# One block for attention and experts, with four row buffers

## The reference, cut to what matters

```
xn = layernorm(x)
s  = attention(xn)        # two causal softmaxes per head, subtracted with weight lambda; RMS norm; @ wo.T
g  = silu(experts(xn))    # top 2 of 8: gate/up (256 -> 512), clipped, gated, down (256 -> 256), weighted sum
out = x + s * g
```

## Time and profile before

| | us |
|---|---|
| median of three runs | 1023.85 (1023.36 to 1024.76) |
| the profiled execution, its own time | 1022.34 |
| its span, first to last instruction | 1020.6 |
| block 1, to about | 160 |
| attention, to the last copy of its results | 743.2 |
| experts, to the last ys (L1684) | 974.95 |
| last stage, to | 1020.6 |

### The profile page before, as it was taken

How to read it: one execution, slowest core, us unless ns; L and a number is a source line. 1 busy time by engine, 2 the same in 40 slices (tenths; PEclk the granted TensorE clock), 3 DMA queues, 4 the chain that set the end, 5 groups by cost and what they waited for, 6 DMA issues and landing times.

```text
span 1020.6 us, 23981 instructions
## 1 busy us (share of the span) xinstructions
PE 907.0 (89%) x6614; PEld 641.3 (63%) x6614; DVE 886.8 (87%) x1743; ACT 768.3 (75%) x2011; POOL 283.0 (28%) x481
## 2 busy tenths in 40 slices
PE   4999985889989899989988898898879999999987
PEld 3877763666666666666666666666646665555676
DVE  6687867999999999999999999999848887778847
ACT  3545435999999999999999999999835555464443
POOL 3000001323332333333200000001146666656610
PEclk9999995999999999999999999999989999999999
DMA  6989966485667758575685556474013333333278
GB/s 209 334 317 314 288 249 187 100 190 139 144 153 173 166 116 185 140 149 139 141 109 125 122 106 141 86 151 92 7 54 120 113 113 99 107 97 106 79 229 287
DMA packets 89553, 157.54 MB, mean 154 GB/s; under 512 B 19580, under 2 KB 48764, under 8 KB 89468
## 3 DMA queue, kind: packets, MB, share of 16 engines
q1 hardware_dynamic: 80544, 137.56, 52.2%
q0 software_dynamic: 8960, 19.41, 6.3%
HBM read 104.57 MB, written 52.36 MB: 154 GB/s over the span
## 4 chain that ended last, share of the span: by engine, by line
PE 33%; DVE 23%; ACT 13%; issue 12%; ACTq 1%; another core or an unknown queue 0%; DVEq 0%; DMA 0%; POOL 0%; POOLq 0%
PE bank L1461 11%; DVE Pr_long L1241 7%; DVE nmax L1191 7%; PE bank L1021 6%; PE bank L1487 5%; ACT Pr_long L1124 4%; DVE nmax L1209 4%; ACT Pr_short L1138 4%; ACT AT L1151 3%; PE bank L1062 2%; PE bank L1528 2%; PE bank L1447 1%; PE bank L1474 1%; PE bank L1023 1%; DVE nmax L1203 1%
## 5 line engine op out<-in xcount | busy, mean ns | idle before, releaser
L1191 DVE TENSOR_REDUCE nmax<-bank 128x1 f32<-128x1024 f32 (+3 forms) x256 | 259.9, 1015 | 5.8 <-PE bank L1023 5.8
L1124 ACT ACTIVATE Pr_long<-bank,nmax 128x1024 f32<-128x1024 f32 (+3 forms) x256 | 252.2, 985 | 9.9 <-DVE nmax L1191 9.8
L1151 ACT COPY AT<-bank 128x512 f32<-128x512 f32 (+3 forms) x384 | 177.3, 494 | 4.3 <-PE bank L1062 2.4
L1021 PE MATMUL bank<-Ks_first,Qs_first 128*128 128x512 f32 (+3 forms) x384 | 123.9, 412 | 28.1 <-ACT Pr_short L1138 18.6
L1138 ACT ACTIVATE Pr_short<-bank,nmax 128x128 f32<-128x128 f32 (+3 forms) x256 | 138.5, 541 | 10.1 <-DVE nmax L1209 2.6
L892 POOL COPY VO<-Ob 128x64 f32 (+1 forms) x128 | 30.2, 236 | 414.3 <-ACT Ob L1160 413.9
L1062 PE MATMUL bank<-ident,Pr_long 128*128 128x128 f32 x832 | 127.9, 280 | 18.3 <-DVE Pr_long L1241 18.2
L1461 PE MATMUL bank<-gu_sb,xsT 128*128 x284 | 135.8, 601 | 4.5 <-ACT xsT L1549 2.7
L1021 PE MATMUL bank<-Ks_second,Qs_second 128*128 128x512 f32 (+3 forms) x384 | 119.2, 399 | 20.7 <-ACT Pr_short L1138 18.5
L1241 DVE SCALAR_TENSOR_TENSOR Pr_long<-Pr_long,coef 128x1024 f32<-128x1024 f32 (+3 forms) x128 | 137.4, 1074 | 0.0
L1023 PE MATMUL bank<-maskb,identb 128*128 128x128 bf16 x512 | 117.8, 233 | 0.0
(11 more groups left out here) (171 smaller groups left out, 1607.3 us busy)
## 6 DMA issues: line engine op xcount, KB each, us to landing
q_parts<-PARTS SPq DMA_DIRECT2D x32, 512.0 KB, 3.1
k_parts<-PARTS SPq DMA_DIRECT2D x32, 512.0 KB, 3.9
Qs_first<-q_parts SPq DMA_DIRECT2D x64, 256.0 KB
Ks_first<-k_parts SPq DMA_DIRECT2D x64, 256.0 KB
Qs_second<-q_parts SPq DMA_DIRECT2D x64, 256.0 KB
Ks_second<-k_parts SPq DMA_DIRECT2D x64, 256.0 KB
X<-x SPq DMA_DIRECT2D x8, 512.0 KB, 5.6
xn_dram<-XN SPq DMA_DIRECT2D x8, 512.0 KB, 6.5
```

The lines of the kernel that those rows point to most:

```text
L1021: nc.tensor.matmul(at[:, c0:c1], Qs[head][:, m, q * P:(q + 1) * P], Ks[head][:, m, c0:c1], start=True, stop=(c1 < N))
L1124: nc.scalar.activation(long_probs(p)[:, m, 0:N], long_slot[m][:, 0:N], ACT.Exp, bias=nmax[:, 4 * p + m:4 * p + m + 1], scale=1.0, accum_ou ...
L1151: nc.scalar.copy(AT[u % 6][:, 0:w], tb[u % BANKS][:, 0:w]).then_inc(unit_out, 1)
L1191: nc.vector.tensor_reduce(nmax[:, 4 * p + m:4 * p + m + 1], long_slot[m][:, 0:N], AX.X, ALU.max, negate=True).then_inc(long_maxed, 1)
```

## The change

- `no_rows` is laid out for four buffers: its iota writes 18 partitions of 8192 words instead of 36 of 4096. It and the iota of `row_ids` move behind GpSimd's other constants.
- Blocks 2 and 3 become one block. The code of block 3 moves into functions (`experts_sp`, `experts_pool`, `experts_pe`, `experts_act`, `experts_dve`) that are called where each engine's attention code ends; their bodies are the same but for what follows.
- In the last iteration TensorE turns the rows of tiles 0 and 1 behind pair 5's frame, runs gate_and_up(0) behind pair 6's and gate_and_up(1) behind pair 7's; ScalarE copies both tiles' turned rows behind pair 6's frame and runs the first gate_curve behind pair 7's. GpSimd fetches the rows of tiles 1 to 3 behind its copy for pair 5.
- Four buffers `xs` and four `ys` in the place of two; AHEAD is 7. A store of ys is waited for four tiles later, and not at all for the first four; the two dummy loads go.
- d1e is computed in the step of tile 1. The Silu table is loaded behind the first three `turned_out`.

The diff, cut; lines that only move are left out.

```diff
-AHEAD = 5
+AHEAD = 7
+ROW_BUFS = 4
+Y_ROWS = TOP_K * T + ROW_BUFS * P
...
-            no_rows = sb("no_rows", [SLOT_TILES // 2, 2 * P, ID_WORDS], I32, where=ph)
+            no_rows = sb("no_rows", [SLOT_TILES // ROW_BUFS, ROW_BUFS * P, ID_WORDS], I32, where=ph)
...
                     nc.gpsimd.tensor_copy(identb[:], ident[:]).then_inc(consts_done, 1)
-                    nc.gpsimd.iota(no_rows[:], pattern=[[1, 2 * P], [0, ID_WORDS]], base=TOP_K * T, channel_multiplier=0
-                                   ).then_inc(no_rows_ready, 1)
-                    nc.gpsimd.iota(row_ids[:], pattern=[[P, NT], [T, TOP_K]], base=0, channel_multiplier=1
-                                   ).then_inc(no_rows_ready, 1)
...
                     nc.gpsimd.tensor_scalar(count_128, count_f[:, 0:T // P], float(P), None, ALU.mult
                                             ).then_inc(consts_done, 1)
+                    nc.gpsimd.iota(no_rows[:], pattern=[[1, ROW_BUFS * P], [0, ID_WORDS]], base=TOP_K * T, channel_multiplier=0
+                                   ).then_inc(no_rows_ready, 1)
+                    nc.gpsimd.iota(row_ids[:], pattern=[[P, NT], [T, TOP_K]], base=0, channel_multiplier=1
+                                   ).then_inc(no_rows_ready, 1)
...
                 for p in range(NP):
                     frame(NIT - 1, p)
+                    behind(p)
...
+            xs = [xs_first] + [sb(f"xs{u}", [P, D], where=ph) for u in range(1, ROW_BUFS)]
...
+            ys = [sb(f"ys{u}", [P, D], where=ph) for u in range(ROW_BUFS)]
...
+                    def rows_in(n):
+
+                        if n >= ROW_BUFS:
+                            pool.wait_ge(xs_turned, 2 + n - ROW_BUFS + 1)
+                        u = n % ROW_BUFS
+                        pool.indirect_dma_start(xs[u][:], None, xn_dram, bass.IndirectOffsetOnAxis(
+                            slot_tokens[:, n:n + 1], 0)).then_inc(xs_loaded[u], 16)
+
+                    if begin:
+
+                        pool.wait_ge(long_scored, credited(NIT - 1, 2 * NP, 2 * NP - 1))
+                        pool.wait_ge(short_scored, credited(NIT - 1, 2 * NP, 2 * NP - 1))
+                        for n in range(1, ROW_BUFS):
+                            rows_in(n)
+                        return
...
+                def first_rows_turned(pe):
+                    pe.wait_ge(ew_loaded, 64 * E)
+
+                    pe.wait_ge(long_exped, credited(NIT - 1, 2 * NP, 2 * NP - 1))
+                    turn_rows(0, 0)
+                    turn_rows(0, 1)
+
+                def experts_pe(pe, load):
+
+                    pe.wait_ge(short_exped, credited(NIT - 1, 2 * NP, 2 * NP - 1))
+                    pe.wait_ge(unit_out, credited(NIT - 1, UNITS, UNITS - 1))
+                    turn_rows(0, 2)
+                    turn_act(0, 0)
+
+                    pe.wait_ge(o_out, credited(NIT - 1, NP, NP))
...
+                    run_steps(pe, step, load, begun=True)
...
+                    for c in range(W_SETS):
+                        turned_out(c)
+
+                    nc.scalar.activation(silu_table[:], ident[:, 0:1], ACT.Silu)
...
+                    m = 2 * it + u
+                    if m == 0:
+                        nc.vector.wait_ge(pv_done, credited(NIT - 1, NP, NP))
+                    if m >= ROW_BUFS:
+                        nc.vector.wait_ge(y_stored[m % ROW_BUFS], 16 * (m // ROW_BUFS))
...
                             pool.indirect_dma_start(xs_first[:], None, xn_dram, bass.IndirectOffsetOnAxis(
                                 slot_tokens[:, 0:1], 0)).then_inc(xs_loaded[0], 16)
+                        if p == 5:
+                            experts_pool(pool, True)
...
                     keep_rows(NIT - 1, NP)
+                    experts_pool(pool, False)
...
+                    def behind(p):
+
+                        if p == NP - 3:
+                            first_rows_turned(pe)
+                        if p == NP - 2:
+                            first.append(load(0))
+                            gate_and_up(0, 0, first[0])
+
+                    run_pairs(pe, 4, frame, behind)
+                    gate_and_up(0, 1, first[0])
                     pe.wait_ge(o_out, credited(NIT - 1, NP, NP - 1))
                     sum_rows(NP - 1).then_inc(pv_done, 1)
+                    experts_pe(pe, load)
...
+                    def behind(p):
+                        if p == NP - 2:
+                            first_rows_out(act)
+
+                    run_pairs(act, 4, frame, behind)
+                    gate_curve(0, 0)
                     act.wait_ge(pv_done, credited(NIT - 1, NP, NP))
                     act.wait_ge(o_kept, credited(NIT - 1, NP, NP - 2))
                     nc.scalar.copy(Ob[0][:, P:], ob[:, P:P + 2 * DH]).then_inc(o_out, 1)
+                    experts_act(act)
```

792 lines of the change are left out of this document (386 added, 406 removed).

## The result

The changed kernel takes 1033.19 us (median of 4 runs, 1032.33 to 1033.97), the kernel before beside it 1023.61 (4 runs, 1021.98 to 1024.76): ratio 1.0095, 95% interval 1.0077 to 1.0112. It is slower by 9.6 us, where 1.9 had been forecast and 1028.8 us was the end of the range. The profiled execution has a span of 1032.2 us against 1020.6, so the trace has 11.6 us to explain.

The account below looks back on a forecast made before the run. No single bound: GpSimd's iota holding VectorE delays the start; TensorE bounds the expert stage and paces the last. +5.1 - 1.5 + 0 - 1.7 = +1.9 on 1023.85 gave 1025.7 us, range 1020.8 to 1028.8.

Parts of the forecast that it names:

- Step 1: Kernel start: the longer iota holds VectorE until 15.7, so XN is ready at 17.4 instead of 12.29; +5.1 us.
- the two bounds of the iota: Kernel start: 8.7 us if words of one partition count, 4.4 us if all words do; 8.7 was taken.
- Rivals B and C: Kernel start: iota costs by all words, sum -2.4, chance 0.08; or VectorE is not held, sum -6.2, chance 0.09.
- Step 2: Seam between attention and experts: the new order gains despite some 3 us waiting; -1.5 us, bounds -3.0 to +1.2.
- the term for the clock: Seam: one half-clock stretch costs up to 1.7 us; -2.2 at full clock became -1.5, nearer to no such stretch.
- rival A: Seam: wait for tile 1's rows ahead of pair 6, then two half-clock stretches; +1.2 there, sum +4.6, chance 0.16.
- Step 3: Expert stage: four row buffers and AHEAD 7 change nothing, since TensorE's own work is the chain; 0 us.
- rival D: Expert stage: four buffers hide late stores seen as unknown-queue waits; -3.7, sum -1.8, chance 0.05.
- Step 4: Last stage: Silu table load moved behind the first three turned chunks; -1.7 us, from -0.3 to a cap of -2.35.
- this 1.5 may go too: Last stage: first projections took 5.16 us instead of 3.62 at half clock; less idle time might remove this.

Follow-up runs that it names:

- rows1_early: Changed kernel with tile 1's rows fetched after pair 3 into the dead first V tile; ratio 0.9961 to the kernel before.
- second pair: Kernel before and changed kernel, both unchanged, profiled again on chip 12; ratios 0.9977 and 1.0007 to the kernel before.
- before_third: The kernel before, unchanged, run again on chip 2; 1022.54 us, ratio 1.0001.

## Why the prediction was wrong

**Step 1 was right**, mechanism and size: +5.1 forecast, +5.0 measured, and the choice between the two bounds of the iota (words per partition, not all words) was confirmed at three shapes. VectorE's tensor_scalar of 0.17 to 0.25 us took 8.16, 7.43, 4.02 and 0.97 us beside an iota and ended with it. Rivals B and C fall. The Trainium skill ("GPSIMD Engine Reference", Extended-addressing connectivity) has each of GpSimd's cores work on its own 16 partitions in an iota; the three durations agree. The Trainium skill ("SBUF — State Buffer", Who interferes with whom) lets a GpSimd instruction block VectorE's two-port modes, which tensor_scalar has and tensor_tensor has not; the traces agree, with the tensor_tensor at 7.32 not held.

**Step 2 was wrong in sign, right in mechanism.** -1.5 was forecast; the seam measured -0.2 here and -0.2 to +1.0 in all pairs, and the part ahead of it +0.9 here (-0.1 to +1.0 in the pairs), of which 0.5 is at attention's first scores (167.54 - 17.39 against 162.03 - 12.40), which the sum didn't have. The wait for tile 1's rows was foreseen (some 3 us; measured 3.52). What failed is the term for the clock: I took one stretch at half clock as unlikely and two as rival A, because no row showed a busy stretch at half clock that another follows. The trace shows 10.3 us at half clock, 744.8 to 755.1; in it gate_and_up(0) took 3.63 us instead of 1.98, which is 1.65 of the loss. rows1_early prices the wait and its clock together at 7.1 us; without them the seam is 49.71 us against 55.88 of the kernel before in that session, and these 6.2 us are what the overlap could have brought. At this place rival A was the right case.

**Step 3 is the step that failed.** "Fetches and stores are no longer among what TensorE waits for in steady state", 0 us: the step took the stage as TensorE's own work, with nothing beside it to wait for, and gave it no bounds but 0. The stage came out 8.65 us longer in the first pair, and -0.6 and +2.8 in the two other pairs profiled on one chip each. Of the 8.65, 7.0 are tiles stretched by late completions (22 increments over 0.5 us late instead of 10), and 1.7 is half clock at tile 51. With this term at its value of the first pair and the others at theirs the sum is +11.6, with all terms of the second pair about +2. The size depends on the chip and the session: a stage without late completions takes 212.3 to 213.2 us, the longest took 226.74, of which 1.7 is again the clock. The profile of before had it in sight: two rows of an unknown queue, 3.70 us. I read them as possible late stores and gave rival D 0.05 because 67 other tiles had none; in truth ten increments were late, and only the two longest show in the chain. What the record supports is this: in such a session completions come late at places that differ from one execution to the next, so the expert stage's length has a spread of its own, and it belongs in the range. Whether the change itself adds to it (theory M, some 3 us) stays open. Nor is the step's 0 the worth of the four buffers: at the seam of the one block two buffers cost 6.3 to 6.6 us, which the forecast had nowhere.

**Step 4 was right in direction and short in size.** -1.7 with a cap of -2.35; the tail gained 2.7, and 4.5 to 4.6 in the other two pairs. The load is worth 1.0 us; the term that was missized is again the clock, which I had named ("this 1.5 may go too") and then kept out of the cap. The Trainium skill ("ScalarE: Activation LUTs", What ACT_TABLE_LOAD costs) adds a drain of 1.38 us to each table load. The traces here don't show it: in before_third the load starts 0.01 us behind the operation before it, ends at 978.42, and the next ACT operation starts at 978.44.

**The whole.** Over four sessions the changed kernel was 1.0095, 1.0007, 1.0032 and 1.0063 of the kernel before. The forecast's +1.9 us lies between the two lowest. Where it comes near it is by luck: in the second pair the seam was 2.5 us above its term and the tail 2.9 below. The range was too narrow, since it held the bounds of the steps and not the spread of the expert stage, which the same kernel shows between sessions.

## What to carry to other kernels

A wait put into an in-order queue ahead of other work costs its own length and then the clock that TensorE loses by standing still: here 3.5 us of waiting made 7.1. So move the fetch, and put the operation that waits for it behind the work that is ready; the first was worth the 7.1 us, the second some 3 more where the last increment came late. An iota on GpSimd should be laid over all 128 partitions (1.33 us instead of 8.66 for the same words), the more so where VectorE has a short chain beside it. And where the chain of before holds rows of an unknown queue, profile both kernels on more than one chip, and one of them twice, before the stage is called unchanged.

## What the runs showed that I had not expected

- TensorE's completions reached ACT and VectorE up to 2.2 us late. In the expert stage 8 to 28 increments were over 0.5 us late in each of the fourteen profiles on chips 2, 8 and 12 and of the first pair that have all their transfers, and none in the four on chip 7. Leaving out either the indirect fetches or the indirect stores ended it there, but for one of 0.64 us; in attention, beside the sort's stores alone, 23 or 24 increments stayed 0.64 to 0.91 us late.
- The increments of one fetch can come apart by 2 us: fifteen by 734.60 and the last at 736.64, fifteen by 735.77 and the last at 737.68, both times with a 16 KB instruction packet that started while the fetch landed.
- TensorE stayed at half clock for 10.3 us around one stand of 3.5 us, for the last part of it while fully busy. Behind a stand of 2.1 us at tile 51 the clock fell to half for 3.4 us in nine profiles and not in eleven; no run shows why.
